# A graph-attention kernel's step orders: set-up cut finer, first and last batches written out, the middle reordered

## The reference

```
h = relu(layernorm(x))
# block 1: four attention heads, then one more head on their concatenation ("back")
Wh = h @ W;  e[i,j] = leaky(Wh[i].a1 + Wh[j].a2), masked by adj
head = elu(softmax(e) @ Wh)
out = elu(attention(concat(4 heads), W_out, a_out, adj))
x = x + layernorm(relu(out @ w1 + b1) @ w2 + b2 + out) * gamma + beta
# block 2: graph convolution
h = relu(layernorm(x))
x = x + deg * (h @ Wi.T + b) + adj @ (h @ Wj.T)
```

## Time and profile before

| | us |
|---|---|
| runs (3) | 1412.38, 1413.06, 1413.7 |
| median | 1413.06 |
| the profiled execution | 1413.76 |
| its span, first to last instruction | 1412.0 |
| TensorE busy | 1318.9 |
| mean granted TensorE clock | 0.981 of full speed |

### The profile page before, as it was taken

One profiled execution on the slowest core, in us unless ns is written; L12 is line 12 of the kernel. 1 busy time (PEld: TensorE's weight loads), 2 busy tenths in 40 slices (PEclk: granted clock), 3 DMA queues, 4 the chain that ended last, 5 costly groups with the idle time before them and its releaser, 6 DMA issues.

```text
span 1412.0 us, 27480 instructions
## 1 busy us (share of the span) xinstructions
PE 1318.9 (93%) x10024; PEld 1248.7 (88%) x10024; DVE 1097.5 (78%) x2841; ACT 1109.4 (79%) x2123; POOL 346.7 (25%) x234
## 2 busy tenths in 40 slices
PE   3689999999999999999999999999999999999874
PEld 3689898999999899999989999998999999899763
DVE  6997888787878878787887878788787878778442
ACT  3688987888888788887878878788887878888531
POOL 0021322314122231412223141222314122231411
PEclk9799999999999999999999999999999999999997
DMA  4211001011110101111020111102001110101000
GB/s 164 91 38 44 26 21 56 17 31 46 38 46 20 57 16 31 46 39 46 20 58 16 31 46 38 47 17 61 16 31 46 39 46 16 46 16 31 24 30 15
DMA packets 42741, 55.14 MB, mean 39 GB/s; under 512 B 2864, under 2 KB 30832, under 8 KB 42480
## 3 DMA queue, kind: packets, MB, share of 16 engines
q1 hardware_dynamic: 42608, 53.39, 12.5%
HBM read 44.83 MB, written 8.55 MB: 38 GB/s over the span
## 4 chain that ended last, share of the span: by engine, by line
PE 66%; DVE 17%; ACT 11%; issue 6%; DMA 1%; POOL 0%; POOLq 0%; SPq 0%; ACTq 0%
PE ps L781 45%; PE ps L850 6%; PE ps L950 5%; PE ps L914 4%; PE ps L902 4%; DVE arg L701 3%; DVE arg L675 3%; ACT arg L479 2%; ACT elu L499 2%; DVE prob_lo L652 2%; DVE xb L742 2%; ACT arg L475 1%; DVE h2T_lo L652 1%; DVE zneg L683 1%; ACT prob_hi L485 1%
## 5 line engine op out<-in xcount | busy, mean ns | idle before, releaser
L398 POOL TENSOR_TENSOR hx_lo<-elu,hx_hi 128x512 fp32r<-128x512 f32 x128 | 177.3, 1385 | 867.2 <-ACT hx_hi L508 867.2
L781 PE MATMUL ps<-prob_hi,whx_hi 128*128 128x256 f32 x1024 | 301.6, 295 | 3.6 <-DVE prob_lo L652 3.6
L781 PE MATMUL ps<-prob_hi,whx_lo 128*128 128x256 f32 x1024 | 291.2, 284 | 0.0
L781 PE MATMUL ps<-prob_lo,whx_hi 128*128 128x256 f32 x1024 | 291.0, 284 | 0.0
L499 ACT ACTIVATE elu<-ps 128x512 f32<-128x512 f32 x160 | 94.4, 590 | 174.3 <-PE ps L781 174.3
L479 ACT ACTIVATE arg<-arg,nmax 128x512 f32<-128x512 f32 x320 | 226.6, 711 | 3.9 <-DVE nmax L686 3.8
L475 ACT ACTIVATE arg<-arg,fcol 128x512 f32<-128x512 f32 x320 | 211.9, 712 | 3.1 <-DVE gmax L675 3.1
L675 DVE CUSTOM_DVE_ANT_0 arg<-f2bc,mask 128x512 f32<-128x512 f32 x320 | 207.2, 684 | 5.4 <-DMA f2bc<-f_rows 5.4
L652 DVE TENSOR_TENSOR prob_lo<-ps,prob_hi 128x1024 fp32r<-128x1024 f32 x160 | 195.1, 1219 | 19.4 <-ACT prob_hi L485 17.8
L781 PEld LDWEIGHTS ps<-prob_hi,whx_hi 128*128 128x128 f32 x1024 | 197.5, 193 | 10.6 <-issue 5.9
L781 PEld LDWEIGHTS ps<-prob_hi,whx_lo 128*128 128x128 f32 x1024 | 197.6, 193 | 3.7 <-issue 3.6
(11 more groups left out here) (130 smaller groups left out, 3184.3 us busy)
## 6 DMA issues: line engine op xcount, KB each, us to landing
f2bc<-f_rows SPq DMA_DIRECT2D x80, 256.0 KB, 3.2
xin<-in_x SPq DMA_DIRECT2D x16, 512.0 KB, 5.0
xb<-in_x SPq DMA_DIRECT2D x16, 512.0 KB, 3.9
out_x<-xb SPq DMA_DIRECT2D x16, 512.0 KB, 2.9
f_rows<-f2row SPq DMA_DIRECT2D x80, 2.0 KB
ff<-in_L_gnn_a_heads SPq DMA_DIRECT2D x1, 1024.0 KB, 8.0
arg<-in_adj SPq DMA_DIRECT2D x1, 1024.0 KB, 10.2
ff<-in_L_gnn_W_out SPq DMA_DIRECT2D x1, 1024.0 KB, 7.5
```

Of the source, the lines that this page charges most:

```text
L398: pool.tensor_tensor(out=hx[1][:, 2 * c.h:2 * c.h + 2, c.u * HN:(c.u + 1) * HN], in0=elu[:, c.buf, :, :], in1=hx[0][:, 2 * c.h:2 * c.h + 2 ...
L781: i = pe.matmul(out, a, b_, start=(k == 0), stop=(k == n - 1))
```

## The change

The tables are replaced by three texts for each engine: `FIRST`, a list of steps with their batches, written out for the start; `ROUND`, the middle's order, run for eight rounds; and `LAST`, written out with batches counted from the end. The middle's order on every engine is a new one, and the steps that a round holds for each batch are the same. Set-up changes in these parts:

- `wh_prep` on DVE is split: `wh_low` makes the low part of the weights, `wh_prep` only the dot products.
- `mask` works on half of the tiles at a time. The count of each row goes to ACT (a copy with a running sum) and `mask_end` on DVE finishes each half. ACT's part stands ahead of its `gc_turn` and `turn_in`.
- `wo_prep` is eight steps on DVE, one for each 128 rows of W_out; `brow` is a step of its own. `load_wo` goes ahead of the first `f2send`, and `load_adj` ahead of the second `f2bcast`.
- `adj_cast` with its row sums and `adj_turn`'s copies go from DVE to ACT.

The diff, cut; old and new step lists of the other engines and batches are left out:

```diff
-SP_STEPS = [
...
-PE_STEPS = [
-    ("conv_in", 1, 4), ("m1", (0, 1), 1), ("attend", 3, 2), ("turn_p", 5, 3), ("attend", 4, 3), ("turn_p", 6, 2),
-    ("m1", (1, 0), 1), ("f2turn", 0, 1), ("attend", 5, 3), ("adj_turn", 0, 2), ("conv", 0, 4), ("attend", 6, 2),
-    ("turn_out", 0, 3), ("turn_p", 7, 2), ("m1", (1, 1), 1), ("turn_p", 8, 2), ("ffn1", 0, 3), ("attend", 7, 2),
-    ("gc_turn", 0, 1), ("attend", 8, 2), ("f2turn", 1, 1), ("turn_p", 9, 2), ("m1", (2, 0), 1), ("ffn2", 0, 3),
-    ("adj_turn", 1, 2), ("m1", (2, 1), 1), ("attend", 9, 2), ("turn_p", 0, 1), ("mix2", 0, 2), ("mix2", 1, 2),
-    ("mix2", 2, 2), ("mix2", 3, 2), ("m1", (3, 0), 1), ("turn_p", 1, 1), ("f2turn", -1, 2), ("attend", 0, 1),
-    ("m1", (3, 1), 1), ("turn_p", 2, 1), ("f2turn", 2, 1), ("attend", 1, 1), ("turn_in", 0, 0), ("turn_gc", 0, 3),
-    ("attend", 2, 1), ("f2turn", 3, 1), ("turn_p", 3, 1), ("conv_in", 0, 3), ("m1", (0, 0), 0), ("turn_p", 4, 2),
-]
...
+ROUND_FROM, ROUNDS = 8, 8
+FIRST = {
+    "SP": """
+    load@0 load@1 load_wo@0 f2send:0@0 f2bcast:0@0 f2send:1@0 load_adj@0 f2bcast:1@0 load@2 f2send:2@0 f2bcast:2@0 f2send:3@0
...
+    "PE": """
+    turn_in@0 gc_turn@0 m1:00@0 m1:01@0 m1:10@0 f2turn:0@0 m1:11@0 f2turn:1@0 m1:20@0 m1:21@0 m1:30@0 m1:31@0 turn_p:0@0
+    f2turn:2@0 adj_turn:0@0 adj_turn:1@0 turn_p:1@0 turn_in@1 attend:0@0 attend:1@0 f2turn:3@0 turn_p:2@0 m1:00@1 turn_p:3@0
+    m1:01@1 attend:2@0 f2turn:0@1 attend:3@0 turn_p:6@0 m1:10@1 m1:11@1 turn_p:7@0 attend:6@0 turn_p:8@0 m1:20@1 attend:7@0
...
+    "ACT": """
+    wh_prep:0@0 wh_prep:1@0 wh_prep:2@0 norm_in_out@0 wh_prep:3@0 mask:0@0 gc_turn@0 turn_in@0 m1:00@0 m1:01@0 mask:1@0
+    m1:10@0 wo_prep:0@0 f2turn:0@0 m1:11@0 m1:20@0 m1:21@0 f2turn:1@0 m1:30@0 norm_in_out@1 m1:31@0 args:0@0 args:1@0
+    probs:0@0 f2turn:2@0 adj_cast@0 args:2@0 adj_turn:0@0 probs:1@0 adj_turn:1@0 turn_in@1 args:3@0 elu_neg:0@0 elu_exp:0@0
+    elu_neg:1@0 elu_exp:1@0 hx:0@0 probs:2@0 f2turn:3@0 m1:00@1 probs:3@0 hx:1@0 m1:01@1 args:6@0 elu_neg:2@0 f2turn:0@1
...
+    "DVE": """
+    norm_in@0 norm_in_out@0 wh_low:0@0 wh_low:1@0 wh_low:2@0 wh_prep:0@0 wh_prep:1@0 wh_prep:2@0 mask:0@0 wh_low:3@0
+    wh_prep:3@0 mask_end:0@0 turn_in@0 mask:1@0 norm_in@1 gc_turn@0 m1:00@0 mask_end:1@0 norm_in_out@1 m1:01@0 m1:10@0
+    wo_prep:0@0 wo_prep:1@0 m1:11@0 wo_prep:2@0 wo_prep:3@0 wo_prep:4@0 wo_prep:5@0 rowmax:0@0 wo_prep:6@0 wo_prep:7@0
+    rowmath:0@0 rowmax:1@0 rowmath:1@0 rinv:0@0 m1:20@0 scale:0@0 m1:21@0 m1:30@0 rowmax:2@0 m1:31@0 rinv:1@0 rowmath:2@0
+    scale:1@0 probs:0@0 rowmax:3@0 rinv:2@0 brow@0 probs:1@0 rowmath:3@0 turn_in@1 scale:2@0 rinv:3@0 elu_out:0@0 scale:3@0
+    elu_out:1@0 probs:2@0 rowmax:6@0 rowmath:6@0 m1:00@1 m1:01@1 probs:3@0 rowmax:7@0 rowmath:7@0 rinv:6@0 elu_out:2@0
+    scale:6@0 rowmax:8@0 rinv:7@0 rowmath:8@0 scale:7@0 elu_out:3@0 probs:6@0 rowmax:9@0 m1:10@1 rinv:8@0 scale:8@0 m1:11@1
+    probs:7@0 rowmath:9@0 rowmax:0@1 elu_out:6@0 rinv:9@0 scale:9@0 probs:8@0 rowmax:1@1 elu_out:7@0 m1:20@1 probs:9@0
+    elu_out:8@0 rowmath:0@1 norm_in@2 rinv:0@1 scale:0@1 m1:21@1 elu_out:9@0 rowmath:1@1 rowmax:2@1 rowmath:2@1 rinv:1@1
+    rowmax:3@1 scale:1@1 probs:0@1 rowmath:3@1 mix2:0@0 rinv:2@1 scale:2@1 m1:30@1 rinv:3@1 norm_in_out@2 mix2:1@0 probs:1@1
...
+ROUND = {
...
+    "PE": """
+    m1:31@5 turn_in@4 attend:1@5 f2turn:2@5 turn_p:2@5 m1:00@4 turn_gc@7 m1:01@4 turn_p:3@5 attend:2@5 conv_in:0@7 f2turn:3@5
+    conv_in:1@7 turn_p:4@6 attend:3@5 m1:10@4 turn_p:5@6 attend:4@6 f2turn:0@4 turn_p:6@5 attend:5@6 conv@7 m1:11@4 turn_p:7@5
+    turn_out@6 attend:6@5 ffn1@6 turn_p:8@5 attend:7@5 m1:20@4 turn_p:9@5 f2turn:1@4 attend:8@5 m1:21@4 ffn2@6 m1:30@4
+    attend:9@5 turn_p:0@4 mix2:0@5 mix2:1@5 turn_p:1@4 mix2:2@5 mix2:3@5 attend:0@4 f2turn:-1@5
+    """,
+    "ACT": """
+    probs:9@6 f2turn:1@5 m1:20@5 args:0@5 elu_neg:8@6 hx:7@6 elu_exp:8@6 m1:21@5 hx:8@6 args:1@5 m1:30@5 elu_neg:9@6
+    elu_exp:9@6 probs:0@5 hx:9@6 norm_ff_out@7 norm_in_out@4 args:2@5 probs:1@5 args:3@5 mix2:0@6 mix2:1@6 elu_neg:0@5
+    elu_exp:0@5 f2turn:-1@6 norm_gc_out@7 m1:31@5 turn_in@4 hx:0@5 elu_neg:1@5 f2turn:2@5 elu_exp:1@5 probs:2@5 hx:1@5 m1:00@4
+    turn_gc@7 m1:01@4 probs:3@5 args:4@6 elu_neg:2@5 elu_exp:2@5 conv_in:0@7 args:5@6 f2turn:3@5 probs:4@6 conv_in:1@7
+    args:6@5 elu_neg:3@5 elu_exp:3@5 m1:10@4 hx:2@5 probs:5@6 elu_neg:4@6 elu_exp:4@6 hx:3@5 args:7@5 probs:6@5 elu_neg:5@6
+    f2turn:0@4 elu_exp:5@6 m1:11@4 args:8@5 turn_out@6 probs:7@5 args:9@5 elu_neg:6@5 elu_exp:6@5 probs:8@5 hx:6@5 ffn1@6
+    elu_neg:7@5 elu_exp:7@5
+    """,
+    "DVE": """
+    elu_out:1@6 probs:2@6 m1:00@5 turn_gc@8 rowmax:4@7 rowmath:4@7 m1:01@5 rowmax:5@7 probs:3@6 rinv:4@7 rowmath:5@7 scale:4@7
+    rowmax:6@6 elu_out:2@6 conv_in:0@8 rowmath:6@6 rinv:5@7 scale:5@7 probs:4@7 conv_in:1@8 rowmax:7@6 rinv:6@6 rowmath:7@6
+    scale:6@6 elu_out:3@6 m1:10@5 probs:5@7 norm_in@4 elu_out:4@7 rowmax:8@6 rinv:7@6 scale:7@6 probs:6@6 elu_out:5@7 conv@8
+    rowmath:8@6 m1:11@5 rowmax:9@6 rinv:8@6 rowmath:9@6 scale:8@6 probs:7@6 rowmax:0@5 norm_in_out@4 elu_out:6@6 rinv:9@6
+    scale:9@6 probs:8@6 elu_out:7@6 rowmath:0@5 rowmax:1@5 m1:20@5 rowmath:1@5 probs:9@6 rinv:0@5 scale:0@5 elu_out:8@6
+    m1:21@5 ffn2@7 norm_ff@7 rowmax:2@5 norm_ff_out@7 rinv:1@5 rowmath:2@5 elu_out:9@6 m1:30@5 probs:0@5 scale:1@5 rowmax:3@5
+    rowmath:3@5 x2@7 norm_gc@7 probs:1@5 mix2:0@6 mix2:1@6 rinv:2@5 scale:2@5 norm_gc_out@7 rinv:3@5 scale:3@5 elu_out:0@5
+    m1:31@5 turn_in@4
+    """,
...
+LAST = {
...
+    mix2:0@-2 mix2:1@-2 mix2:2@-2 mix2:3@-2 m1:30@-1 turn_p:1@-1 attend:0@-1 m1:31@-1 f2turn:-1@-2 attend:1@-1 f2turn:2@-1
+    turn_p:2@-1 turn_gc@-3 turn_p:3@-1 attend:2@-1 conv_in:0@-3 conv_in:1@-3 turn_p:4@-2 f2turn:3@-1 attend:3@-1 turn_p:5@-2
+    attend:4@-2 turn_p:6@-1 attend:5@-2 conv@-3 attend:6@-1 turn_out@-2 turn_p:7@-1 turn_p:8@-1 ffn1@-2 attend:7@-1
...
+    rinv:9@-1 scale:9@-1 elu_out:7@-1 probs:9@-1 elu_out:8@-1 ffn2@-2 norm_ff@-2 elu_out:9@-1 norm_ff_out@-2 mix2:0@-1 x2@-2
+    norm_gc@-2 mix2:1@-1 norm_gc_out@-2 turn_gc@-2 rowmax:4@-1 rowmath:4@-1 rowmax:5@-1 rowmath:5@-1 rinv:4@-1 scale:4@-1
...
+        def parse(text):
+
+            for word in text.split():
+                step, at = word.split("@")
+                name, _, which = step.partition(":")
+                if name == "m1":
+                    info = (int(which[0]), int(which[1]))
+                else:
+                    info = int(which) if which else 0
+                yield name, info, int(at)
...
-        def steps(table):
-
-            for t in range(B + LATEST):
-                for name, info, late in table:
-                    if 0 <= t - late < (1 if name in ONCE else B):
+        def steps(engine):
+
+            for name, info, b in parse(FIRST[engine]):
+                yield name, info, b
+            for t in range(ROUND_FROM, ROUND_FROM + ROUNDS):
+                for name, info, late in parse(ROUND[engine]):
+                    if 0 <= t - late < B:
                         yield name, info, t - late
+            for name, info, b in parse(LAST[engine]):
...
                 sp.wait_ge(s_pick, 1)
+                sp.wait_ge(s_wh_lo, H)
...
-                sp.wait_ge(s_wo, 1)
+                sp.wait_ge(s_wo, OC)
                 sp.dma_start(adj_f.bitcast(i32), adj.rearrange("(c p) n -> p c n", p=P)).then_inc(ld[LD_ADJ2], 16)
...
+            def mask_(c):
+
+                act.wait_ge(s_edges, c.info + 1)
+                for n in (2 * c.info, 2 * c.info + 1):
+                    i = act.activation(mask[:, n, :], mask[:, n, :], ACT.Copy, accum_out=cnt[:, n:n + 1])
+                i.then_inc(s_counted, 1)
+
+            def adj_cast(c):
+
+                act.wait_ge(ld[LD_ADJ2], 16)
+                for n in range(NC):
+                    i = act.activation(adj_f[:, n, :], adj_f[:, n, :].bitcast(i32), ACT.Copy, accum_out=deg[:, n:n + 1])
+                i.then_inc(s_adj, 1)
+
+            def adj_turn(c):
+                act.wait_ge(s_adj_turned, c.info + 1)
+                for i in range(2):
+                    n = 2 * c.info + i
+                    r = act.activation(adjT[:, :, n * P:(n + 1) * P], pairs[c.pair][:, i, :].rearrange("p (j i) -> p j i", j=NC), ACT.Copy)
+                r.then_inc(s_adj_out, 1)
...
                 h = c.info
+                dve.wait_ge(ld[LD_A], 16)
                 dve.wait_ge(ld[LD_WH], 16 * KC)
-                dve.wait_ge(ld[LD_A], 16)
                 for k in range(KC):
                     for z in range(2):
                         i = dot(w_heads[k][:, h, :], a_h[:, h, z, :], wsum[:, k, h, z:z + 1], 2 * k + z)
                 link(i)
                 link(dve.tensor_copy(wh[0][:, :, h, F:FA], wsum[:, :, h, :]))
+                dve.tensor_tensor(out=wh[1][:, :, h, F:FA], in0=wsum[:, :, h, :], in1=wh[0][:, :, h, F:FA].bitcast(fp32), op=ALU.subtract).then_inc(s_wh, 1)
+
+            def wh_low(c):
+                h = c.info
```

(72 more changed lines are left out.)

267 lines of the change are left out of this document (209 added, 58 removed), and 3 rows, old and new, of the table SP_STEPS.

## The result

The changed kernel takes 1399.1 us, median of 4 runs (1393.1 to 1399.8), the kernel before 1413.4 (four runs): ratio 0.989, 95% interval 0.9862 to 0.9918. In run 1 four more runs of the same instructions gave 1391.7 to 1393.5 (median 1392.4, ratio 0.9852, interval 0.9838 to 0.9866). Forecast: 1395, range 1384 to 1408. The profile is of the 1393.1 us run. The three other runs of those four were 6 us longer at a mean granted clock of 0.980 to 0.981 instead of 0.984, and none of them was profiled; run 2 shows a place where such an amount can arise.

What follows compares the result with a forecast made beforehand. Middle bound by PE, the loss at the ends; gains of 12.4 (middle), 4.4 (start), 1.2 (drift after it) and 0.5 us (tail) sum to 18.5, from 1413.76 to 1395.3, said as 1395, range 1384 to 1408.

Steps and rivals of the forecast that it cites:

- The two waits: Middle: PE's waits for PSUM evictions, 0.58 us at attend:4 (L742) and 0.87 at conv (L652), both go.
- Tight places: Middle: attend:1, turn_gc and attend:8 have only 2.3 us after an attend, met by 0.1 to 0.2 us.
- Middle in all: Middle batches: 19.4 us of PE waits go, less 7.0 for DVE meeting POOL at tight places, 12.4 us gained.
- (a): Start, first m1: at 22.0 us instead of 16.30, 5.7 us late, behind the mask work on DVE and ACT.
- (e): Start, payback: DVE free of wo_prep and adj work; same work done at 104.4 us instead of 108.8, gain 4.4.
- (c): Start, SP: f2bcast:1 behind load_adj takes 5.9 us, rowmax:2 waits 1.5 us for it.
- (f): From 135 to 152 us: four waits like the middle's, 2.5 us in all, half counted as gain, 1.2 us.
- Tail: End: 0.87 us gained at turn_gc@14, 0.4 lost at turn_p:3@15, last layer norm's 15.89 us stay; gain 0.5.
- 2 and 5: 2: a tight place missed once per batch, 1403, chance 0.17; 5: DVE late at all three each batch, 1433, 0.09.
- Rival 4: Middle: DVE as late at other takers, 1.45 us a batch stays, only the ends count; 1408 to 1411, chance 0.06.
- Rival 1: Clean round without a new wait, start at its better side (+9); 29 us gained, 1385, chance 0.12.
- rival 3: Start gives nothing: f2bcast:1 lands late, wo_prep holds the first attends; -3 instead of 4.4, 1402, chance 0.08.

Runs made afterwards that it cites:

- run 1: The changed kernel again, its orders written out as one list per engine (same instructions): median 1392.4 us.
- run 2: Set-up and orders of the kernel before up to about 140 us, the changed kernel's middle and end behind: 1412.8 us.
- run 5: Kernel before with two DVE moves in its round, probs:6 ahead of rowmax:8 and conv_in:1 ahead of rinv:6 and scale:6: 1390.1 us.
- run 9: Changed kernel with two swaps of neighbours, elu_exp:1 ahead of f2turn:2 on ACT, elu_out:4 ahead of norm_in on DVE: 1393.3 us.
- Run 6: Changed kernel with the first batch's turn_in ahead of mask:0 on DVE, and ahead of mask:0 and gc_turn on ACT: 1390.4 us.
- run 10: Changed kernel with the first batch's f2bcast:1 ahead of load_adj on SP: 1395.3 us.
- run 8: Changed kernel with two more GpSimd subtractions, waited for by nobody, behind each hx_lo: 1419.5 us.

## Why the prediction was right, point by point

- **The two waits go**: right, and their cause too (evictions queued on DVE), as run 5 shows on the old round alone. The new order was not needed for it. Mis-sized was the floor: the prediction took 81.05 us of busy time as PE's work, and it is 80.57. The most that the order could give was 1.9 us a batch and not 1.45.
- **Tight places**: of the three named, turn_gc waits, for a reason that the prediction did not have: an ACT step that waits for a DMA between the two halves of an ELU, 0.40 us a round. conv was not named, with 0.8 us to spare, and there the mechanism of the prediction is at work, by the rows of run 9: a meeting with POOL makes norm_in 2.8 us long, where the walk has 1.96, and all that was to spare is gone (0.33 us a round). Meetings also come in every round and not in every second (rowmax at 586.95 us takes 2.87 us instead of 0.69), but the others stand where nobody waits.
- **Middle in all**: 12.4 us forecast, of which 0.56 for the single wait in the last middle batch; 15.2 measured for the thirteen pairs. The floor was 0.47 us a batch too high, 6.1 in all. 7.0 us were charged for new waits, and 9.8 are missing to the floor of 80.57: 5.8 in the seven rounds, 1.4 and 1.9 in the two long periods named above, and small rests. The two errors cancel in part; that the total fits is partly luck.
- **Start, (a) to (e)**: first m1 22.0 walked and 22.12 measured, turn_p:0 47.8 and 48.50, adj_turn:0 53.7 and 54.18, attend:0 59.1 and 60.50, attend:3 73.2 and 75.77, mix2:0 100.5 and 100.78. The walk was up to 2.6 us short on the way and met the end again. The same work is done at 104.5 us instead of 108.8: 4.3 where 4.4 was forecast. f2bcast:1 took 6.2 us from issue to rowmax, forecast 5.9. Run 6 shows that (a) cost 1 to 2 us of its 5.8, run 10 that (c) is worth 1 us at most.
- **(f)**: 0.3 us (4.6 less 4.3) instead of 1.2.
- **Tail**: 0.8 us (20.7 less 19.9) instead of 0.5, the 2.7 behind the last turn_in being for the most part the thirteenth pair. The h2T_lo step did what it should, a wait of 2.37 us for 3.20, and the distance from turn_gc to conv_in there fell by 1.7: the other 0.9 is clock, 0.67 of full speed in that stretch instead of 0.50 (the eight transposes take 1.09 us instead of 1.97), which nothing in the walk foresaw. The single wait of 0.56 us gave 0.4, and turn_p:3 lost 1.1 where 0.4 was charged. The 15.9 us of the last layer norm stand.
- **Rivals**: 2 and 5 are real as a mechanism (run 8, and conv in every round), and at the middle's POOL load of 21 us a period they do not decide. Rival 4 is excluded by the period. Rival 1 wanted a round without a new wait, and there are two; rival 3 a start that gives nothing, and it gave 4.3.
- **The total**: 1395.3 against 1393.1 in the profiled run and 1392.4 in run 1, and 1399.1 in the median of the first four. That the 6 us between them fall inside the range is no merit of the walk.

## What to carry to other kernels

Before a round is reordered, look at what the waited-for instruction stands behind on its own engine: two moves of a DVE step ahead of others that had time gave 24 us, at least as much as a new order of everything. In these traces a wait row is a lower bound of what the wait costs, and a busy row an upper bound of the work; the distance between two step starts shows both. A long busy row of a small step is a wait too: it is found by comparing the row with the same step elsewhere. An order written out for one stretch can't be joined to another's without a look at the waits behind the seam, and the gain of a shorter period can end behind a transfer that was in time before.

## What the runs showed of the hardware

- A PE wait for a PSUM pair cost 0.16 and 0.24 us more than its row (1.03 and 0.82 us of step distance for waits of 0.87 and 0.58). The rows show why for the first: matmuls of an attend last 0.28 us and start 0.12 apart, and the one behind a wait starts after the whole 0.28.
- A 128x256 dot of two SBUF tiles on DVE takes 0.94 us beside a GpSimd subtraction that itself grows from 0.64 to 0.90, and 0.41 alone: by the rows they take turns, one whole instruction each. Even a 128x2 step (0.16 us) stands for the rest of a 2.40 us GpSimd one, and a 128x4 TENSOR_SCALAR (0.17 us) takes 1.00 beside a hx_lo and ends with it.
- Behind PE waits of 3.54 and 5.64 us at the same attend the granted clock was 0.62 and 0.54 of full speed over the next 4.5 and 5.0 us, between the two levels; behind 1.17 us the attend took its usual 2.95 us.
- A 256 KB broadcast issued behind a 1 MB load landed 6.1 us after its issue, with 3.2 us as the usual time and 3.0 in run 10, where it goes out first.
